# Edge orders by a bitonic network on VectorE, and edge rows gathered from a packed table

## The reference

```python
x = ln(x + L0(x, edges))      # 4 message rounds; sums over src (row = src)
x = ln(x + L1(x, edge_attr_64, edge_attr_9, edges))   # attention over dst
x = ln(x + L2(x, edges, edge_attr_16))                # messages, sum over dst
x = ln(x + L3(x, edges))                              # normalized sum over dst
# L0, one round:
m = silu(silu(concat(h[src], h[dst]) @ w1 + b1) @ w2 + b2)
agg = segment_sum(m, src)
# L1, per edge factors, needed for all edges and independent of x:
wk = relu(e64 @ k_w1 + k_b1) @ k_w2 + k_b2
wv = relu(e64 @ v_w1 + v_b1) @ v_w2 + v_b2
```

## Time and profile before

| | us |
|---|---|
| median of 3 runs | 11473.12 (11461.88 to 11473.56) |
| span of the profiled execution | 11517.6 |
| POOL busy | 7536.3 (65%) |
| PE busy | 8528.8 (74%) |
| DVE busy | 5781.3 (50%) |
| ACT busy | 2487.6 (22%) |

### The profile page before, as it was taken

The page is one execution under the profiler, slowest core; times in us unless marked ns, Lnnn a source line. Parts: engine busy times, 40 slices in busy tenths (PEclk is TensorE's granted clock), DMA queues, the critical chain, the costliest instruction groups (busy, mean ns, idle before and its releaser), DMA issues. The chain is left out here.

```text
span 11517.6 us, 188628 instructions
## 1 busy us (share of the span) xinstructions
PE 8528.8 (74%) x45085; PEld 7091.0 (62%) x45086; DVE 5781.3 (50%) x14752; ACT 2487.6 (22%) x4616; POOL 7536.3 (65%) x7547
## 2 busy tenths in 40 slices
PE   4677588867777877777777778999996667884333
PEld 2565344456666666566666667888885566773333
DVE  9775000034443444344444447888888744443333
ACT  0001234311111111111111114555554711110000
POOL 5777777767766776677667764555553557775776
PEclk5555788867777777777777778999998978885555
DMA  1333344331213211321122117888886422221111
GB/s 31 89 109 107 107 143 137 133 65 51 51 43 81 52 51 43 81 52 52 43 72 52 51 41 214 254 253 254 254 252 161 141 48 62 62 61 24 26 26 26
DMA packets 854761, 1110.04 MB, mean 96 GB/s; under 512 B 337331, under 2 KB 531544, under 8 KB 853398
## 3 DMA queue, kind: packets, MB, share of 16 engines
q1 hardware_dynamic: 306058, 473.67, 14.4%
q0 software_dynamic: 264160, 418.34, 13.3%
q10 hardware_dynamic: 284332, 215.58, 7.2%
HBM read 898.41 MB, written 208.50 MB: 96 GB/s over the span
## 5 line engine op out<-in xcount | busy, mean ns | idle before, releaser
L1207 POOL DMA_INDIRECT gx_l<-xr,gi_l x4160 | 4041.5, 972 | 1695.8 <-issue 902.6
L1316 DVE TENSOR_TENSOR aggT_l<-aggT_l,psum 64x128 f32 x4160 | 1159.0, 279 | 875.5 <-DVE aggT_l L1316 721.3
L1887 POOL DMA_INDIRECT gx<-xr,gi x832 | 899.3, 1081 | 970.9 <-DVEq L1976 415.0
L1899 PE MATMUL psum<-cw,xa 128*128 128x256 f32 x6656 | 1510.6, 382 | 16.7 <-DVE xa L1985 10.1
L1329 DVE TENSOR_TENSOR pre_s_l<-psum,gx_l 128x512 f32<-128x512 f32 x520 | 359.4, 691 | 2156.0 <-DMA gx_l<-xr,gi_l 2132.0
L1899 PEld LDWEIGHTS psum<-cw,xa 128*128 128x128 f32 x6656 | 1233.7, 190 | 232.1 <-issue 79.1
L1372 PE MATMUL psum<-ptab,oht 128*128 x6656 | 1159.0, 347 | 289.7 <-issue 239.8
L1372 PEld LDWEIGHTS psum<-ptab,oht 128*128 128x128 f32 x6656 | 1099.3, 258 | 382.7 <-issue 380.7
L927 POOL DMA_INDIRECT slots_s<-rec_s,row_s x806 | 821.3, 1019 | 408.7 <-issue 341.3
L1956 ACT COPY xT<-psum 32x512 f32<-32x512 f32 x1664 | 957.8, 576 | 289.7 <-PE psum L1924 272.8
L2511 POOL DMA_INDIRECT gx_l<-xr,gi_l x832 | 785.5, 944 | 321.1 <-issue 177.3
(11 more groups left out here) (375 smaller groups left out, 12236.5 us busy)
## 6 DMA issues: line engine op xcount, KB each, us to landing
wkv<-slots_d ACTq DMA_DIRECT2D x208, 568.0 KB, 6.6
kr<-keyrow_s SPq DMA_DIRECT2D x416, 256.0 KB
shb<-shT SPq DMA_DIRECT2D x1664, 64.0 KB
gx_l<-xr,gi_l POOLq DMA_INDIRECT x4992, 2.4
vtab<-kv ACTq DMA_DIRECT2D x208, 256.0 KB
v_in<-vtab SPq DMA_DIRECT2D x104, 512.0 KB, 3.3
hT<-noderow SPq DMA_DIRECT2D x101, 512.0 KB
kr<-keyrow_d SPq DMA_DIRECT2D x208, 128.0 KB
```

Of the source, the lines that this page charges most:

```text
L1207: pool.indirect_dma_start(gx[j][:, c_, :], None, xr, bass.IndirectOffsetOnAxis(ap=gi[j][:, c_:c_ + 1], axis=0)).then_inc(rows_in[j][h].sem ...
L1316: ins = dve.tensor_tensor(a, a, sums(j, h), ALU.add)
L1887: pool.indirect_dma_start(gx2[r][:, t, :], None, xr2, bass.IndirectOffsetOnAxis(ap=gi1[j][:, t:t + 1], axis=0)).then_inc(rows_in1[r][h].se ...
L1899: ins = pe.matmul(bank[2 + p][:, t % 2 * OKV:(t % 2 + 1) * OKV], xa[j][:, c, t * P:(t + 1) * P], cw[:, c, :], start=c == 0, stop=c == KC - 1)
```

## The change

Both orders are now made by sorting. An entry is one 32-bit word, an exponent bit (`ABOVE`), the target and the edge's number for order "d", the source and the target for order "s", compared as a float. With padding entries for each block, 128 × 1024 entries are sorted by a bitonic network. In it DVE compares within lanes (`within`, L451 and L452, one minimum and one maximum over 512 columns) and, for distances of 128 entries and above, in a transposed form (`across`, L448 and L449 with a sign, else L451 and L452), between which PE transposes the table (8 blocks, L508) and ACT copies it back (L517 to L522): 15 such rounds in a sort, 153 compare steps.

Meanwhile all edges are packed in memory. For each of 26 groups of 31 columns SP loads the 64, 9 and 16 features into one of three buffers, ACT copies the 64 (L572), POOL writes the source, the two target numbers and the 25 other features (L579 to L584), and SP stores rows of 92 floats to `erow`. After the sort by target the sorted edge numbers, `edge_at`, say which edge belongs to a slot. POOL gathers the rows (L855, 832 indirect DMAs), the factor loop runs in slot order (208 turns), ACT copies both parts to `eo`, and SP stores `eo` densely. The sort for order "s" runs on DVE during the gathers; its rounds stand in the factor loop's PE and ACT code at fixed turns, and its keys and indices are formed by DVE with no trip to memory but the keys' row. The scatters, `ranks_s_*`, `totals_*`, `places_*`, the pattern fills and the record copies are gone.

```diff
-        def scatter_s_pool():
...
-        def scatter_d_pool():
...
+        def network_dve(o):
+            def compare(a, b, lo, hi, negated=False, last=True):
+                if negated:
+                    dve.scalar_tensor_tensor(lo, b, -1.0, a, ALU.mult, ALU.min)
+                    ins = dve.scalar_tensor_tensor(hi, b, -1.0, a, ALU.mult, ALU.max)
+                else:
+                    dve.tensor_tensor(lo, a, b, ALU.min)
+                    ins = dve.tensor_tensor(hi, a, b, ALU.max)
+                if last:
+                    step(ins)
...
+            for k in range(10):
+                within(2 ** k, mirrored=k > 0)
+                for j in range(k - 1, -1, -1):
+                    within(2 ** j)
+            for m in range(1, 8):
+                turn_over(2 * m - 2)
+                for half in range(2):
+                    dve.wait_ge(net_kept.sem, kept_by(o, 2 * m - 2, half))
+                    across(m, m - 1, slice(half * CN // 2, (half + 1) * CN // 2), True, half == 1)
...
+                for j in range(m - 2, -1, -1):
+                    across(m, j, slice(0, CN), False, True)
...
+                turn_over(2 * m - 1)
+                dve.wait_ge(net_kept.sem, kept_by(o, 2 * m - 1, 1))
+                for j in range(9, -1, -1):
+                    within(2 ** j)
...
+        def pack_pool(g):
...
+            if g >= STAGED:
+                pool.wait_ge(staged_out[j].sem, out_by[g - STAGED])
+            pool.tensor_copy(r[:, :, D + F_OTHER], src[:, cols])
+            pool.tensor_copy(r[:, :, D + F_KEY], low_d[:, cols])
+            pool.tensor_copy(r[:, :, D + F_NODE], dst[:, cols])
+            pool.wait_ge(staged_in[j].sem, staged_loads(g))
+            pool.tensor_copy(r[:, :, D + F_SH:D + F_SH + S], sh_in[j][:])
+            fields_set.at(pool.tensor_copy(r[:, :, D + F_ATTR:D + F_ATTR + A], attr_in[j][:]))
...
+        packed_first = 10
...
+            network_act("d", r)
+            if r % 2:
+                for g in range(g, min(g + 2, NG)):
+                    pack_act(g)
...
+        def gather_edges_pool():
+            for j in range(STAGED):
+                pool.wait_ge(staged_out[j].sem, staged_out[j].n)
+            pool.wait_ge(empty_out.sem, empty_out.n)
+            pool.wait_ge(edges_found.sem, edges_found.n)
...
+                if i >= AHEAD:
+                    pool.wait_ge(e_turned.sem, i - AHEAD + 1)
+                    pool.wait_ge(e_out.sem, i - AHEAD + 1)
...
+                    e_loaded[j][t // PAIR].at(pool.indirect_dma_start(
+                        ein[j][:, t, :], None, erow,
+                        bass.IndirectOffsetOnAxis(ap=edge_at[:, i * EW + t:i * EW + t + 1], axis=0)), 16)
...
+        count_at, keys_at = 8, 160
+            rounds_at[24 + 8 * m] = 2 * m - 2
+            rounds_at[24 + 8 * m + 4] = 2 * m - 1
```

More of the change, by code:

```diff
@@ L66 @@
 AW = H * (HD + 1) + 1
-EC8 = -(-EC // W) * W
+RW = D + FD
+EMPTY = P * EC - NE
+EW = 4
+NF = TILES["d"] // EW
+FAR = {o: struct.unpack("f", struct.pack("I", 0x7F000000 + first))[0] for o, first in (("d", NE), ("s", N))}
+assert TILES["d"] % EW == 0 and 32 <= EMPTY and N + 63 < NPAD
 KQ = 16
@@ L409, in offsets_dve @@
-            gb_done.at(dve.tensor_reduce(gb[:, 0:GC], hit[:, 0:GC, 0:NB - 1], AX.X, ALU.add))
-        def blocks_pe(o):
-            pe.wait_ge(gb_done.sem, gb_done.n)
-            for h in range(-(-TILES[o] // (PER[o] * P))):
-                ins = pe.matmul(PS[0:1, 6 * 512 + h * P:6 * 512 + (h + 1) * P], gb[:, h:h + 1], ident[:], start=True, stop=True)
-            gb_rows.at(ins)
-        places_ready, placed = [], sig("placed")
-        ranked = [rank, pos]
-        early, rest = slice(0, FIRST), slice(FIRST, EC)
@@ L484, in ends_dve @@
-        def ends_dve():
-            step(dve.tensor_scalar(tile_ends[:], gend[0:1, :], -1.0, 0.0, ALU.add, ALU.max))
-        def ends_sp(at):
-            sp.wait_ge(done.sem, at)
-            sp.wait_ge(filled_d.sem, filled_d.n)
-            sp.nop(nofuse=True)
-            for b in range(0, NB, CH):
-                last = nc.values_load_multi_w_load_instructions(
-                    tile_ends[0:1, b:b + CH], engines=[sp.engine], min_val=0, max_val=TILES["d"] - 1,
-                    skip_runtime_bounds_check_because="a block's last tile lies before the end of the table")[1]
-                for t_ in last:
-                    filled_d.at(sp.dma_start(wide_rows[:, bass.ds(t_, 1), :], pattern[:].unsqueeze(1)), 16)
@@ new lines, in offsets_dve, with blocks_pe, blocks_dve @@
+            gb_done.at(dve.tensor_reduce(gb[:], hit[:, :, 0:NB - 1], AX.X, ALU.add))
+        def blocks_pe(at):
+            pe.wait_ge(gb_done.sem, at)
+            pe.nop(nofuse=True)
+            for h in range(7):
+                ins = pe.matmul(PS[0:1, 4 * 512 + h * P:4 * 512 + (h + 1) * P], gb[:, h:h + 1], ident[:], start=True, stop=True)
+            gb_rows.at(ins)
+        def blocks_dve(o, turned):
+            dve.wait_ge(gb_rows.sem, turned)
+            step(dve.tensor_copy(blk[o][:], PS[0:1, 4 * 512:4 * 512 + 7 * P]))
@@ L734, in build @@
+        for g in range(g, NG):
+            pack_act(g)
+        staging.close()
+        ein = [tmp(f"ein{j}", [P, EW, RW]) for j in range(AHEAD)]
         einT = [tmp(f"einT{j}", [D, EW * P]) for j in range(2)]
@@ L1123, in build @@
         factor_act()
[L1124 to L1133 removed]
+        factor_sp()
         pre.close()
```

880 lines of the change are left out of this document (344 added, 536 removed).

## The result

| | us |
|---|---|
| before, median of 4 runs | 11473.34 |
| after, median of 4 runs (10665.25 to 10680.37) | 10672.26 |
| ratio | 0.9305, 95% interval 0.9291 to 0.9318 |
| span of the profiled execution after | 10663.1 |

A forecast was written before the change was run, and what follows sets the result against it. POOL's two chains of 806 scatters bound the preparation, 2330.7 us. New preparation 335 + 1090 + 29 + 46 + 22 = 1522 us, layers +15: −794 us, span 10724, scaled to a median of 10680 us; range 10590 to 10840 us.

The forecast's parts named there:

- network starts: Start of the target sort's compare steps on DVE, after counting, signs, entries, offsets and blocks: about 49 us.
- steps and rounds, no copies beside: Target sort: 153 compare steps on DVE, 210 us, plus fifteen handovers to PE and back, 39 us.
- POOL's copies beside DVE: During the target sort, POOL's packing copies slow DVE: 26 us, the middle of bounds 0 and 58 us.
- end of packing: Behind the target sort, the last two ACT copies (4 us) and a store's issue and landing (about 6 us): 11 us.
- start stall: Start of the edge gathers: POOL, four groups ahead, waits for PE and ACT, which first do the node work: 29 us.
- 832 gathers with contention: Edge gathers on POOL at 1.31 us each, 1090 us, plus 46 us for the source sort's DVE operations lengthening them.
- drain: From the last edge gather's start through landing, PE, ACT and store to the first layer gather: 22 us.
- layers: Gathered rows become spread in the source-ordered layers: 15 us more, within 0 to 37 us.
- The lock: Rival, 0.12: DVE and POOL exclude each other for whole instructions; DVE loses 58, POOL 76 us; 62 us more, 10740 us.
- Packing: Rival, 0.12: packing the edges bounds the preparation; 75 MB take 357 us, gathers start 45 us later: 10725 us.
- The ring: Rival, 0.12: edge gathers wait for PE, whose groups take 6.15 us each, 1279 us instead of 1136: 10825 us.
- The slower one: Rival, 0.03: spread rows land late, so every source-layer gather pays; at 0.3 us each, +998 us, 11680 us.

The follow-up runs named there:

- early packs: Changed kernel with ACT packing three groups instead of two behind each of the first three odd rounds, none left behind the last: 10681.32 us, ratio 0.9301.
- the two runs with the unsorted entries: Changed kernel without the source sort's compare steps: 11038 us, ratio 0.9606; the same with source layers gathering the source's row, not the target's: 11072.77 us, ratio 0.9639.

## Why the prediction was right

The forecast of 10680 us was 8 us off, and by the right mechanism: two chains of 806 scatters give way to a sort of some 250 us and one chain of 832 gathers. But that it came within 8 us is luck: two errors cancel. Against the profiled execution the sum stood at 10724 us, the trace ends at 10663: 61 us too high (19 at the start of the gathers, 17 in them, 28 in the layers, less 3 in the drain). And the proportion of 0.39%, taken from one execution of the kernel before, brought it down by 44 (exactly, 42, to 10682). By terms:

| step | predicted | measured |
|---|---|---|
| network starts | 49 | 47.1 |
| steps and rounds, no copies beside | to 298 | to 292.7 |
| POOL's copies beside DVE | 26 | 9 to 10 |
| end of packing | 11 | 14.4 from `edge_at`'s start |
| first gather | 335 | 316.3 |
| start stall | 29 | 21 |
| 832 gathers with contention | 1136 | 1127 |
| last gather | 1500 | 1464.5 |
| drain | 22 | 24.9 |
| layers | +15 | -13 in the first traces of the two kernels, +26 in the second |

- **Network.** Right. 157 ns and 1.045 ns a column from the earlier trace rows gave the steps, the rounds, and the whole came out 5 us too high.
- **The lock.** The mis-sized term. "The middle, because DVE is in such an operation most of the time" took 26 of bounds 0 and 58; the runs show 10. The bound of 58 supposed that a copy holds DVE for as long as it takes. The rows show that DVE and POOL do take turns, so the rival has the mechanism right and even its sign appeared (L451 at 0.98 us, longer than 692 ns), but a group holds DVE for far less than 2.2 us: 0.29 and 0.49 us for its two larger copies. The rival's price falls, not its rule.
- **End of packing.** 3 us short; the step was right, but it was worth nothing: with the wait gone, POOL waits for PE in its place.
- **Start stall.** Right in kind. It depends on when PE is free, not on when the gathers start; my sum added the two, and early packs show that only the later one counts.
- **The gathers.** 1.31 us each with 46 us of contention came near the measured 1.35 us for a wrong reason. The second network costs 0 to 11 us at the end of the chain; its sign, gathers near 1.3 us long between 440 and 520 us, did not appear (981 ns in the mean of 58). The difference lies in waits for the pair two back. I had noted such a wait in the layers and gave it no term here; it was in the sum only as far as the row scatter's 1.346 us contains it.
- **Rivals.** Packing was not the bound: ACT's waits for loaded features ended at 98 us, ahead of its copies for the first round at 126. The ring held POOL back for 8 us after the start. The slower one, by late landing, did not happen in this kernel, but the two runs with the unsorted entries show its mechanism: late pairs and the shifted phase that follows cost 0.12 us a gather, 366 us in all.
- **Layers.** Nothing that these runs can tell from zero. The scatter of the layers alone, 9170 to 9200 us, is larger than the term.

## What to carry to other kernels

When a chain is paced by its issuing engine, list everything that the engine waits for per instruction and count it over the chain: 0.14 us a gather for a throttle of two pairs, 117 us in all, gave back 65 us here when it was loosened, more than all the contention argued over. A resource that is late at a hand-over (here the packed rows) is worth only what it is later than the next one (PE, in its node work); move both or neither. And don't scale a sum by one profiled execution: take the difference from stage to stage, and the scatter from a second trace.

## What the runs showed of the hardware

- A comparison on DVE with two SBUF inputs and a POOL copy of SBUF worked in turn: a copy of 279 or 496 elements a lane ended 0.27 to 0.29 or 0.48 to 0.50 us after a comparison, the next comparison of 512 columns 0.52 to 0.55 us after the copy. Rows of both are recorded with their waits (0.91 and 0.98 us instead of 0.69 on DVE, 1.08 instead of 0.62 on POOL), so a sum of recorded durations says little: 70 us of copies cost DVE 10. POOL's indirect DMA that begins in the middle of a comparison of 1024 columns takes 1.53 us instead of 0.94, one that begins 0.15 us ahead of it 1.03.
- A gather whose 128 rows were in part or all one row (by the layout of the entries) landed after 2.8 and 3.5 us, one with each row some 33 times after 2.4, like spread rows.
- The factor loop began at a granted clock of 0.50 (1.2 GHz) in every run of the changed kernel and stayed there for 9, 10, 18 or 25 us before 1.00 (2.4 GHz). The order of PE's work right before doesn't sort these: with only the node products there it was 9, 18 and 25 us, with all of the node work 9 to 18.
